# One clamp per step in the first sequence's threshold search, and 32 columns of the count given to ScalarE

## What is computed

```python
# layer 0: a mask of the 5120 largest entries of a 512 x 512 matrix
adj = emb_s * emb_t                       # (512, 1) * (1, 512)
adj = adj * softmax(x, axis=-1) / sqrt(512)
adj[diag, diag] = -inf
x = x + one_hot_mask(top_k(adj.reshape(-1), 5120))
# layer 1: a transformer block with adaptive layer norm
shift1, scale1, gate1, shift2, scale2, gate2 = split(cond @ ada_w + ada_b, 6)
x1 = ln(x) * (1 + scale1) + shift1
y = x + gate1 * (attention(x1; 16 heads of 128) @ out_w + out_b)
out = x + y + gate2 * (gelu((ln(y) * (1 + scale2) + shift2) @ w1 + b1) @ w2 + b2)
```

## Time and profile before

| | us |
|---|---|
| median of 3 runs | 1705.92 |
| lowest and highest | 1703.39, 1706.01 |
| the profiled execution | 1708.25 |
| its span in the profile | 1706.5 |
| TensorE busy | 1618.6 (95%) |
| VectorE busy | 1165.1 (68%) |
| ScalarE busy | 856.0 (50%) |
| GpSimd busy | 151.8 (9%) |

### The profile page before, as it was taken

How to read it: one execution, slowest core, us unless ns; L and a number is a source line. 1 busy time by engine, 2 the same in 40 slices (tenths; PEclk the granted TensorE clock), 3 DMA queues, 4 the chain that set the end, 5 groups by cost and what they waited for, 6 DMA issues and landing times.

```text
span 1706.5 us, 22502 instructions
## 1 busy us (share of the span) xinstructions
PE 1618.6 (95%) x8268; PEld 1355.0 (79%) x8268; DVE 1165.1 (68%) x2524; ACT 856.0 (50%) x1623; POOL 151.8 (9%) x89
## 2 busy tenths in 40 slices
PE   1759999999999999999999999999999999999998
PEld 1758888888778888888778888888878888888887
DVE  6767877767875877776674887776675667665421
ACT  4445666654834555553652555554472455444240
POOL 5511312214300000000000000000000000000000
PEclk9999999999999999999999999999999999999999
DMA  9813525536556133234345323234345331332453
GB/s 372 280 52 124 178 82 185 186 126 248 207 222 228 50 124 124 70 128 159 149 165 215 133 107 115 75 124 148 148 150 196 148 124 50 123 124 79 169 197 123
DMA packets 63853, 256.32 MB, mean 150 GB/s; under 512 B 4352, under 2 KB 4480, under 8 KB 60800
## 3 DMA queue, kind: packets, MB, share of 16 engines
q1 hardware_dynamic: 63456, 254.56, 40.5%
q10 hardware_dynamic: 288, 0.33, 0.1%
HBM read 200.34 MB, written 54.53 MB: 149 GB/s over the span
## 4 chain that ended last, share of the span: by engine, by line
PE 84%; DVE 10%; ACT 3%; issue 1%; DVEq 1%; DMA 0%; SPq 0%; ACTq 0%
PE bank L1118 24%; PE bank L1120 24%; PE bank L1119 23%; PE bank L1212 6%; DVE tb L803 3%; DVE act L995 1%; PE bank L1238 1%; PE bank L1280 1%; PE bank L1275 1%; PE bank L1142 1%; PE bank L1276 1%; PE bank L1160 1%; DVE prob L971 1%; PE bank L1161 1%; ACT prob L679 1%
## 5 line engine op out<-in xcount | busy, mean ns | idle before, releaser
L1118 PE MATMUL bank<-xT,w 128*128 128x512 f32 x704 | 280.6, 399 | 0.5 <-POOL w L514 0.5
L679 ACT ACTIVATE prob<-bank,nbias 128x512 f32<-128x512 f32 x256 | 176.7, 690 | 201.0 <-DVE nbias L968 200.9
L1120 PE MATMUL bank<-xT,w 128*128 128x512 f32 x704 | 274.8, 390 | 0.0
L1119 PE MATMUL bank<-xT,w 128*128 128x512 f32 x704 | 274.6, 390 | 0.0
L1118 PE MATMUL bank<-act,w 128*128 128x512 f32 (+1 forms) x576 | 217.7, 378 | 0.9 <-DVE act L932 0.8
L1120 PE MATMUL bank<-act,w 128*128 128x512 f32 (+1 forms) x576 | 211.0, 366 | 0.0
L1119 PE MATMUL bank<-act,w 128*128 128x512 f32 (+1 forms) x576 | 210.7, 366 | 0.0
L979 DVE TENSOR_TENSOR probT<-bank,probT 128x512 fp32r<-128x512 f32 x256 | 158.5, 681 | 24.9 <-ACT probT L689 24.8
L962 DVE TENSOR_REDUCE rowmax<-bank 128x1 f32<-128x512 f32 x256 | 174.6, 682 | 0.2 <-issue 0.2
L1120 PEld LDWEIGHTS bank<-xT,w 128*128 128x128 f32 x704 | 132.5, 188 | 27.9
L1118 PEld LDWEIGHTS bank<-xT,w 128*128 128x128 f32 x704 | 132.5, 188 | 26.0 <-POOL w L514 0.9
(11 more groups left out here) (134 smaller groups left out, 3047.5 us busy)
## 6 DMA issues: line engine op xcount, KB each, us to landing
w<-split_weights SPq DMA_DIRECT2D x152, 1024.0 KB, 5.3
split_weights<-w SPq DMA_DIRECT2D x40, 1024.0 KB, 6.1
wraw<-weights_in SPq DMA_DIRECT2D x48, 512.0 KB, 4.1
split_weights<-xT SPq DMA_DIRECT2D x8, 1024.0 KB, 7.7
adaw<-ada_w_in SPq DMA_DIRECT2D x4, 1536.0 KB, 15.8
xr<-x_in SPq DMA_DIRECT2D x4, 1024.0 KB, 6.4
out<-x SPq DMA_DIRECT2D x4, 1024.0 KB, 4.4
adj<-x_in SPq DMA_DIRECT2D x3, 1024.0 KB, 6.9
```

The lines of the kernel that those rows point to most:

```text
L679: nc.scalar.activation(prob[:, i, :], bank[i][:, :], ACT.Exp, bias=nbias[:, i:i + 1], scale=SCALE, accum_out=rowsum[:, i:i + 1]).then_inc( ...
L1118: pe.matmul(dst, w_hi_ap, x_hi_ap, start=first, stop=False)
L1119: pe.matmul(dst, w_hi_ap, x_lo_ap, start=False, stop=False)
L1120: return pe.matmul(dst, w_lo_ap, x_hi_ap, start=False, stop=last)
```

## The change

It concerns the search of sequence 0 alone (`is_t0`). There:

- the total comes out scaled by `BIG` = 2^17 and shifted: the weights of the two matmuls are `big` and `minus_half_big` in bf16, and a third matmul, of `big` and a column `offset`, is done ahead of them. It waits only for the previous move (`cand_ready`), as it writes into the same place of PSUM;
- right behind its count VectorE writes `bounds`, the candidate less and plus half a bit, by a tensor_scalar of two elements per partition on the constants `reach`, and drains;
- the move is then one tensor_scalar: the total, not less than the lower and not more than the upper bound, into `cand`. `step_up` and the drain behind it are gone;
- VectorE counts columns 0 to 991, ScalarE the other 1056;
- GpSimd makes the new constants at the start (4 memsets, and 32 of one column for `reach`), and ScalarE, VectorE and TensorE wait for seven signals of `consts_ready`.

```diff
+BIG = float(1 << (LEVEL + 1))
+FIRST_V, FIRST_S = 992, 1056
+SHORT = P * FIRST_S // 2 - KTOP + 0.5
+CONSTS = 7
+def is_t0(t):
+    return isinstance(t, int) and t == 0
+def count_split(t):
+    return FIRST_V if is_t0(t) else NCOUNT
@@ tiles
+        bounds = new("bounds", [P, 2], F32)
+        reach = new("reach", [P, 2 * LEVEL], F32)
+        big = new("big", [P, P], BF16)
+        minus_half_big = new("minus_half_big", [P, P], BF16)
+        offset = new("offset", [P, 1], F16)
@@ gpsimd, ahead of clear_diagonal(0, ...)
+            for step in range(LEVEL):
+                far = TOP_BIT / (1 << step) / 2
+                nc.gpsimd.memset(reach[:, 2 * step:2 * step + 1], -far)
+                ins = nc.gpsimd.memset(reach[:, 2 * step + 1:2 * step + 2], far)
+            ins.then_inc(consts_ready, 1)
@@ vector, count
-                src = keys16[:, :NCOUNT, 1] if step < LEVEL else low[:, :NCOUNT]
+                end = count_split(t)
+                src = keys16[:, :end, 1] if step < LEVEL else low[:, :end]
                 with nc.allow_low_precision(reason=EXACT):
-                    V.tensor_scalar(passed_v, src, cand[:, :], None, op0=ALU.is_ge, op1=ALU.add,
+                    V.tensor_scalar(passed_v[:, :end], src, cand[:, :], None, op0=ALU.is_ge, op1=ALU.add,
                                     accum_out=cnt_v[:, :]).then_inc(counted_v, 1)
+                if is_t0(t):
+                    at = 2 * (step % LEVEL)
+                    V.tensor_scalar(bounds[:, :], reach[:, at:at + 2], cand[:, :], None, ALU.add)
+                    dve.drain()
@@ vector, topk_move
-                V.tensor_scalar(step_up[:, :], total(step)[:, 0:1], float(KTOP - P * NCOUNT // 2) - 0.5, bit,
-                                ALU.is_gt, ALU.mult)
-                dve.drain()
-                move = V.tensor_scalar(cand[:, :], cand[:, :], step_up[:, :], -bit / 2, ALU.add, ALU.add)
+                if is_t0(t):
+                    move = V.tensor_scalar(cand[:, :], total(step)[:, 0:1], bounds[:, 0:1], bounds[:, 1:2],
+                                           ALU.max, ALU.min)
+                else:
@@ tensor, take_total
+                if is_t0(t) and step:
+                    pe.wait_ge(cand_ready, step + 1)
+                weight_v, weight_s = (big, minus_half_big) if is_t0(t) else (ones, minus_half)
+                if is_t0(t):
+                    pe.matmul(total(step)[:, 0:1], big[:, :], offset[:, :], start=True, stop=False)
                 pe.wait_ge(counted_v, t * STEPS + (step + 1))
                 pe.wait_ge(counted_s, t * STEPS + (step + 1))
-                pe.matmul(total(step)[:, 0:1], ones[:, :], cnt_v[:, :], start=True, stop=False)
-                pe.matmul(total(step)[:, 0:1], minus_half[:, :], cnt_s[:, :], start=False, stop=True)\
+                pe.matmul(total(step)[:, 0:1], weight_v[:, :], cnt_v[:, :], start=not is_t0(t), stop=False)
+                pe.matmul(total(step)[:, 0:1], weight_s[:, :], cnt_s[:, :], start=False, stop=True)\
                     .then_inc(total_ready, 1)
```

More of the change, by code:

```diff
@@ L220, in block_kernel @@
         passed_v = tb[:, :].bitcast(BF16)
-        passed_s = new("passed_s", [P, NCOUNT], BF16)
+        passed_s = new("passed_s", [P, FIRST_S], BF16)
         small = new("small", [P, NCOLS], F32)
@@ L495, in _ @@
             nc.gpsimd.memset(minus_half[:, :], -0.5).then_inc(consts_ready, 1)
+            nc.gpsimd.memset(big[:, :], BIG).then_inc(consts_ready, 1)
+            nc.gpsimd.memset(minus_half_big[:, :], -BIG / 2).then_inc(consts_ready, 1)
+            nc.gpsimd.memset(offset[:, :], float(SHORT // P))
+            pool.drain()
+            nc.gpsimd.memset(offset[0:1, :], SHORT - SHORT // P * (P - 1)).then_inc(consts_ready, 1)
             pool.wait_ge(ident_zero, 2)
@@ L579, in topk_count @@
             def topk_count(t, step):
-                src = keys16[:, NCOUNT:, 1] if step < LEVEL else low[:, NCOUNT:]
+                at = count_split(t)
+                src = keys16[:, at:, 1] if step < LEVEL else low[:, at:]
                 act_e.wait_ge(cand_ready, t * (STEPS + 1) + (step + 1))
                 with nc.allow_low_precision(reason=EXACT):
-                    nc.scalar.activation(passed_s[:, :], src, ACT.Sign, bias=cand[:, :], scale=-1.0,
+                    nc.scalar.activation(passed_s[:, :2 * NCOUNT - at], src, ACT.Sign, bias=cand[:, :], scale=-1.0,
                                          accum_out=cnt_s[:, :]).then_inc(counted_s, 1)
@@ L774, in _ @@
             act_e.dma_start(tb[:, :], cond[0:1, :].to_broadcast([P, T])).then_inc(tb_in, 16)
-            act_e.wait_ge(consts_ready, 3)
+            act_e.wait_ge(consts_ready, CONSTS)
             nc.scalar.activation(table[:, :], ident[:, 0:1], ACT.Exp)
@@ L856, in topk_move @@
                 bit = TOP_BIT / (1 << step % LEVEL)
-                V.tensor_scalar(step_up[:, :], total(step)[:, 0:1], float(KTOP - P * NCOUNT // 2) - 0.5, bit,
-                                ALU.is_gt, ALU.mult)
-                dve.drain()
-                move = V.tensor_scalar(cand[:, :], cand[:, :], step_up[:, :], -bit / 2, ALU.add, ALU.add)
+                if is_t0(t):
+                    move = V.tensor_scalar(cand[:, :], total(step)[:, 0:1], bounds[:, 0:1], bounds[:, 1:2],
+                                           ALU.max, ALU.min)
+                else:
+                    V.tensor_scalar(step_up[:, :], total(step)[:, 0:1], float(KTOP - P * NCOUNT // 2) - 0.5, bit,
+                                    ALU.is_gt, ALU.mult)
+                    dve.drain()
+                    move = V.tensor_scalar(cand[:, :], cand[:, :], step_up[:, :], -bit / 2, ALU.add, ALU.add)
                 if step != LEVEL - 1:
@@ L1098, in _ @@
             topk_keys(0, 0, NT)
+            dve.wait_ge(consts_ready, CONSTS)
             start_level(0, 0)
@@ L1363, in _ @@
             pe.sem_inc(y2_done, Y2_CREDIT)
-            pe.wait_ge(consts_ready, 3)
+            pe.wait_ge(consts_ready, CONSTS)
             c0 = COLS["cond"][0]
```

## The result

The changed kernel takes 1713.24 us in the median of six runs (1712.68 to 1718.79), the kernel before 1705.4 in as many: a ratio of 1.005, with a 95% interval from 1.004 to 1.006, so 7.8 us slower. Forecast were 1712 and a range from 1706.5 to 1717. The profiled execution of the changed kernel took 1713.2 us with a span of 1711.3.

The account below looks back on a forecast made before the run. Sequence 0's threshold search, running ahead of TensorE's first projection, was taken to delay all that follows. Terms -7.7 - 1.1 + 0.2 + 16.7 - 2.1 = +6.0 us on the median 1705.92 gave 1712 us, range 1706.5 to 1717.

Parts of the forecast that it names:

- The step on which it turned: In the search of sequence 0: the two-element bounds instruction waits until GpSimd's running split instruction ends; main case, chance 0.83.
- Removed, 32 x 0.24: Search of sequence 0: step_up and its drain go, 0.24 us per step, -7.7 us; clamp taken at 0.21 us.
- Columns, -1.1: Counts of sequence 0: VectorE counts 32 columns fewer, 0.033 us per count, -1.1 us; ScalarE keeps 0.06 us of lead.
- TensorE, +0.2 with an end at +1.2: Steps 8 to 31: third matmul beside modulation matmuls makes TensorE nearly level with VectorE, +0.2 us, at worst +1.2.
- Start, 0 with an end at +2: Kernel start: 36 more GpSimd memsets and a wait for constants cost 0, or +2 us if narrow memsets aren't short.
- Holds, +16.7 in fifteen steps: Search of sequence 0: GpSimd's weight splits hold bounds, so the clamp comes late in fifteen steps, +16.7 us.
- the walk: Step-by-step replay of the new search through GpSimd's 24 split instructions at their old times, giving the late clamps.
- Between the levels, -2.1: Between the search's two levels: the low instructions come at 63.9, in a gap between splits, -2.1 us.
- The free rival: Search of sequence 0: bounds is never held and stays near 0.2 us; -8 us, 1698 us (1695 to 1702), chance 0.11.

Follow-up runs that it names:

- two of the variants: The changed kernel with bounds written by two one-element tensor_scalars, 1702.9 us, and with bounds as one two-element tensor_scalar in the accumulating form, 1700.4 us.

## Why the prediction was right

The step on which it turned, "a two-element tensor_scalar is held while GpSimd works", is shown: by the added instruction alone (+15.3 us), by one element in its place (none held), by the accumulating form (none held), and by the splits moved away (none held).

*Removed, 32 x 0.24.* Right. But the **clamp was mis-sized**: between 0.16 and 0.26 us were given and 0.21 taken; it takes 0.276 to 0.279, above the upper end, and the next count starts 0.39 behind it, not 0.32. That is 32 x 0.07 = +2.2 us, and one term of the sum less certain than it was put. With one per-partition scalar more than the move and PSUM as its source it takes 0.06 more than the move's 0.214; which of the two costs it was not separated.

*Columns, -1.1.* Right in the search: 1.25 instead of 1.28 us a count, VectorE still last by 0.06.

*TensorE, +0.2 with an end at +1.2.* It isn't level: with the clamp at 0.28 a step is 1.96 us with or without modulation matmuls, 26.16 to 28.12 (step 2) and 86.06 to 88.02. The margin is small: the load of the offset's weights ends at 85.71, and the next load waits for VectorE until 85.80.

*Start, 0 with an end at +2.* Right at 0: 32 narrow memsets start 0.033 us apart and are done at 3.61; the exponential begins at 4.99 (5.02 before).

*Holds, +16.7 in fifteen steps.* 14.3 us in fourteen. Steps 0 and 1 were given 1.94 and 1.52 and came at 1.94 and 1.45. From step 3 on the walk was out of phase, so that it named other steps (6, 11, 18 and 21 were not held, 3, 13 and 19 were). One premise did not hold: "I take GpSimd's 24 instructions where they are now". In the first level they start 0.2 to 0.8 us earlier than before, for instance at 42.49 instead of 43.31. The issue gap of 0.53 us ahead of the count of step 4 is no difference, as the kernel before has one of 0.52 there. I walked the prediction's rules again, as an estimate: with the longer clamp alone the holds are 14.6 us, with the splits of the changed kernel's own trace alone 15.7, with both 14.3. So the rule of the holds is right, and the longer clamp is paid back in part by shorter holds, as a held step starts afresh.

The pair of splits of which that is the second, first before, then in the changed kernel:

```profile
42.19 1.04 POOL L532 CAST xT<-wraw 128x1024 fp32r<-128x1024 f32 x1 [0.45 <-DMA wraw<-weights_in]
43.31 2.35 POOL L534 TENSOR_TENSOR xT<-wraw,xT 128x1024 fp32r<-128x1024 f32 x1
```

```profile
41.37 1.04 POOL L556 CAST xT<-wraw 128x1024 fp32r<-128x1024 f32 x1 [0.32 <-DMA wraw<-weights_in]
42.49 2.34 POOL L558 TENSOR_TENSOR xT<-wraw,xT 128x1024 fp32r<-128x1024 f32 x1
```

*Between the levels, -2.1.* This was the **second mis-sized term**: the place came at 61.05, not at 63.9, within a subtraction (60.67 to 63.02). L905 was held for 1.8 us; from its start to the new candidate it is 5.52 us instead of 5.87, so -0.35. The rule was right, the point in time was not, and that is the splits' doing: the walk with their true starts puts the place at 61.04, with the clamp as predicted or as measured.

Measured terms: -7.7 + 2.2 - 1.1 + 14.3 - 0.35 = +7.4 us, and the `eqm` instruction is 7.06 later, as the search also starts 0.2 us earlier. Against the +6.0 of the prediction the terms are off by +2.2 (clamp), -2.4 (holds), +1.75 (between the levels) and -0.2 (TensorE). The first two belong together as said; that the rest is no more than 1.4 us is also luck. In the medians 7.8 and 8.6 are more than that; moved tiles can add to them, which the changed kernel was not tried without.

*The free rival* is what two of the variants are: search 7.05 and 7.3 us shorter, 1702.9 and 1700.4 instead of the 1698 given. The clamp's 2.2 us take the difference for 1700.4, the granted clock the further 2.5 of the other.

## What to carry over

A small VectorE instruction that looks free in a wait is free only if nothing else can hold it: look up not its duration but what GpSimd does at that moment, and look in the trace for an instruction of the same form and width that met it. Write such helpers one element wide or in the accumulating form. And before a few microseconds are explained, shift the tiles by themselves: here that alone was worth 2.8 us.

## What the runs showed of the hardware that was not expected

- A GpSimd memset, which reads nothing, holds a two-element tensor_scalar to its end as a subtraction does (bounds to 38.23, memset to 38.21), even when it starts 0.07 us later by the profile's start times.
- A two-element tensor_scalar in the accumulating form takes 0.208 to 0.211 us, less than the plain one undisturbed (0.223), and its accumulator read of 0.08 us starts 0.14 us after its own start. It costs the step nothing.
- The one-element clamp from PSUM with two per-partition scalars takes 0.278 us, against 0.159 for `step_up` (PSUM, no per-partition scalar) and 0.214 for the move (SBUF, one).
- Single low stretches of the granted clock behind a pause of TensorE of 1.7 us: down to 0.50 over 2 us, a mean of 0.94 and 0.97 over 820 to 860 us in one profile of the kernel before, 0.91 over 1220 to 1240 in the other, 0.91 over 840 to 860 in the second profile of the changed kernel and none in its first, though it pauses alike. Each is worth 1.8 us.
- 64 bytes more in one tile: 2.8 us in the median of this kernel (1.0011 to 1.0029), and in the profiles 2.7 us more of TensorE's busy time on the same 6151 matmuls.
